# Key and value products of a cross attention made two stages earlier, layer norm statistics inside two loops, and two bias additions exchanged between TensorE and GpSimd, in a 12-stage decoder kernel

## The reference

```python
x = x + L0_attn(_layernorm(x), ...)
x = x + L0_xattn(_layernorm(x), ctx_2048, mask_Bx1xS2_ff0)
x = x + L0_ffn(_layernorm(x), ...)
x = x + L1_attn(_layernorm(x), ...)
x = x + L1_xattn(_layernorm(x), ctx_2048, ...)
...
# L0_xattn: x_dq, w_dq rounded through fp8 with one scale each
out = jnp.einsum('bmk,bkn->bmn', x_dq, w_dq) + bias        # bias: (4, 1, 256)
# L1_xattn, 16 heads of 16
q = x @ Wq + bq
kv = cond @ Wkv + bkv                                      # cond is ctx_2048
q, k = _fq_sym(q * scale, axis=-1), _fq_sym(k, axis=-1)    # rounded to 127 steps per token and head
v = _fq_sym(v, axis=2)                                     # one scale per column over all keys
attn = _fq_unsigned(softmax(q k^T))
return (attn @ v) @ Wp + bp
```

## Time and profile before

| | |
|---|---|
| median of 3 runs | 1985.23 us |
| the profiled execution | 1986.46 us, its span 1985.0 us |
| TensorE, VectorE, ScalarE, GpSimd busy | 78%, 62%, 41%, 35% of the span |
| L0a loop; L0x; L0f | from 63.8 us to 281; to 315; to 362 |
| L1a head, loop | to 382.5; to 637 |
| L1x head, loop | 641.5 to 710.5; to 933.5 |
| all stages behind | 933.5 to 1985 |

### The profile page before, as it was taken

The page is one execution under the profiler, slowest core; times in us unless marked ns, Lnnn a source line. Parts: engine busy times, 40 slices in busy tenths (PEclk is TensorE's granted clock), DMA queues, the critical chain, the costliest instruction groups (busy, mean ns, idle before and its releaser), DMA issues. The chain is left out here.

```text
span 1985.0 us, 26882 instructions
## 1 busy us (share of the span) xinstructions
PE 1538.4 (78%) x8607; PEld 1063.1 (54%) x8610; DVE 1237.6 (62%) x3228; ACT 817.1 (41%) x2164; POOL 702.2 (35%) x968
## 2 busy tenths in 40 slices
PE   4899964799998969996983892044687679948998
PEld 3566643688887513332662461012565469944665
DVE  3587776355555378886237327997788679953222
ACT  1244431244433277775225213212577458821111
POOL 1488840175663156664001003333555322210000
PEclk8799986899999755555986895567799979958999
DMA  5000002100000065554000002101000110000000
GB/s 197 22 7 7 1 12 90 41 7 1 6 1 1 0 106 91 89 90 115 28 1 0 1 1 87 37 0 54 1 1 1 73 57 2 2 0 1 0 0 22
DMA packets 98379, 62.20 MB, mean 31 GB/s; under 512 B 88896, under 2 KB 93376, under 8 KB 96448
## 3 DMA queue, kind: packets, MB, share of 16 engines
q1 hardware_dynamic: 98240, 60.48, 11.4%
HBM read 38.44 MB, written 1.05 MB: 20 GB/s over the span
## 5 line engine op out<-in xcount | busy, mean ns | idle before, releaser
L101 PE MATMUL banks<-arena_a,normed_t 128*128 128x512 f32 (+3 forms) x736 | 283.5, 535 | 11.7 <-PEq L2943 11.7
L421 POOL TENSOR_TENSOR lut_weights<-lut_weights,arena_b 128x536 f32<-128x536 f32 x128 | 179.2, 1400 | 193.4 <-DVE arena_b L411 183.5
L101 PEld LDWEIGHTS banks<-arena_a,normed_t 128*128 128x128 f32 x736 | 141.4, 212 | 123.9 <-issue 120.6
L580 POOL TENSOR_SCALAR work<-work,small 128x256 f32<-128x256 f32 (+1 forms) x384 | 178.1, 482 | 73.7 <-DVE small L572 73.7
L101 PE MATMUL banks<-arena_a 64*128 64x512 bf16 (+1 forms) x384 | 161.6, 539 | 17.8 <-ACT arena_a L1489 11.7
L1489 ACT ACTIVATE arena_a<-banks,work 128x1024 uint8<-128x1024 f32 x128 | 154.1, 1204 | 47.3 <-DVE work L1430 39.5
L1428 DVE TENSOR_REDUCE work<-banks 128x1 f32<-128x1024 f32 x128 | 155.3, 1214 | 26.9 <-PE banks L101 26.9
L1518 POOL TENSOR_SCALAR arena_a<-arena_a 128x1024 bf16<-128x1024 uint8 x128 | 133.1, 1045 | 90.0 <-DMA arena_a<-arena_a 84.8
L107 PE MATMUL banks<-identity,work 128*128 128x128 f32 x968 | 133.7, 279 | 16.8 <-DVE work L1086 11.2
L560 ACT ACTIVATE work<-banks,small 128x256 f32<-128x256 f32 (+1 forms) x258 | 115.2, 458 | 62.5 <-DVE small L547 58.4
L107 PEld LDWEIGHTS banks<-identity,work 128*128 128x128 f32 x968 | 113.3, 146 | 31.4 <-DVE work L1086 12.2
(11 more groups left out here) (407 smaller groups left out, 3437.8 us busy)
## 6 DMA issues: line engine op xcount, KB each, us to landing
arena_a<-in_L3f_wg SPq DMA_DIRECT2D x1, 4096.0 KB, 13.2
arena_b<-in_lut_idx SPq DMA_DIRECT2D x8, 268.0 KB, 2.8
arena_b<-in_L_wqn SPq DMA_DIRECT2D x1, 2048.0 KB, 12.4
arena_b<-in_L_wo SPq DMA_DIRECT2D x1, 2048.0 KB, 17.8
arena_a<-in_L_wq SPq DMA_DIRECT2D x1, 2048.0 KB, 7.5
arena_a<-in_L_wo SPq DMA_DIRECT2D x1, 2048.0 KB, 12.9
arena_a<-arena_a SPq DMA_TRANSPOSE x128, 2.4
arena_a<-in_L_wgu SPq DMA_DIRECT2D x1, 2048.0 KB, 9.7
```

What stands on the lines that cost most here:

```text
L101: ins = t.matmul(out, lhs_t, rhs, start=start and i == 0, stop=stop and i == n - 1)
L421: g.tensor_tensor(o, o, lut_t[j % 2], ALU.add).then_inc(*summed.up(c * LUT + j))
L580: ins = g.tensor_scalar(e[:, c], e[:, c], A.rl[n % 2][:, 2 * hh + i:2 * hh + i + 1], 0.0, ALU.mult, ALU.add)
```

## The change

- The values of L1x are made at the head of L0x (`cross_values_tensor` and `_scalar`), the keys in L0f: batch 0 ahead of its norm, batches 1 to 3 behind its low rank product (`cross_keys_tensor` and `_scalar`). They are kept in `W["vtf"]` and `W["k4"]` (in `work`). So that `work` is free for the keys, L1a's turned probabilities move from `work` to `big_b`.
- The loads of stage 4 are issued in L0a, between the mask's load and the first LUT chunk, no longer in L1a.
- L1x has no key or value products; VectorE reads the keys from SBUF, finds the values' scale behind batch 1's keys and rounds the values behind batch 0's queries; ScalarE rounds the values between the splits of batches 1 and 2.
- In both self attentions `statistics(b)` follows the last addition to batch `b` in the loop; the separate statistics and one barrier go.
- L0x: the addition on GpSimd goes. A one-row float32 matmul opens each tile's product (`row`, a row of ones times the inverse factor, made on VectorE, times a row of `bias1`), 8 in all.
- L1x's loop: the one-row product with `bp4` goes. GpSimd adds `bp4` to a tile of the residual at the fifth item of each 16.

```diff
@@ heads_product_vector
         v.tensor_tensor(x_of(b), A.bank01["y", m].f, x_of(b), ALU.add).then_inc(*out_added.up(A.s, m))
+        if m // 4 == GROUPS - 1:
+            v.wait_ge(*out_added.now())
+            statistics(b)
@@ l0_attention and l1_attention, vector
             yield MEET
-            for b in range(NB):
-                statistics(b)
-            yield MEET
@@ l0_attention, sync
             load(1)
+            load(4)
             yield from lut_sync(chunks)
@@ l0_cross, tensor
+            yield from cross_values_tensor(s)
+            t.wait_ge(*(yield loaded[1], "all"))
             for b in range(NB):
...
+                t.wait_ge(*(yield vs, s, "row"))
+                t.wait_ge(*(yield as_, s, "v", b))
                 t.wait_ge(*(yield xt_a, s, b))
                 for i in range(TB):
...
+                    t.matmul(o, row, W["bias1"][0:1, b * D:(b + 1) * D], start=True, stop=False)
+                    ins = products(t, o, [...], start=False)
@@ l0_cross, vector
-            v.wait_ge(*(yield gs, s, "bias"))
@@ l0_cross, scalar
             yield from norm_scalar(s, nf)
+            yield from cross_values_scalar(s)
@@ new, beside l0_cross
+    def cross_keys_tensor(s, b):
+        if b >= 2:
+            t.wait_ge(*(yield as_, s, "k", b - 2))
+        for i in range(TB):
+            ins = products(t, banks[6 + b % 2].f[:, i * D:(i + 1) * D], with_row(ctx_t, b, i, lambda k: W["wkv4"][:, k * 512:k * 512 + D], W["bk4"]))
+        ins.then_inc(*ts.up(s, "k", b))
+    def cross_keys_scalar(s, b):
+        a.wait_ge(*(yield ts, s, "k", b))
+        a.copy(W["k4"][:, b * CB:(b + 1) * CB], banks[6 + b % 2].f).then_inc(*as_.up(s, "k", b))
@@ l0_ffn, tensor
+            yield from cross_keys_tensor(s, 0)
             yield from norm_tensor(s, nf, low)
...
                 ins.then_inc(*ts.up(s, "low", b))
+            for b in range(1, NB):
+                yield from cross_keys_tensor(s, b)
...
+                    else:
+                        t.wait_ge(*(yield as_, s, "k", c + 2))
@@ l1_cross, tensor
-            for b in range(NB):
-                projected(banks[b].f, ctx_t, b, lambda k: W["wkv4"][:, k * 512:k * 512 + D], W["bk4"]).then_inc(*ts.up(s, "k", b))
...
-                    products(t, banks[z].f, [(W["wkv4"][...], ctx_t[...]) for kk in range(KH)]).then_inc(*ts.up(s, "v", z))
...
-                    products(t, out_bank(i)[:, 0:D], [(ot[i % 2][:, j * P:(j + 1) * P], wp[j]) for j in range(KH)] +
-                             [(ones[0:1, :], W["bp4"][0:1, :])]).then_inc(*out_made.up(s, i))
+                    products(t, out_bank(i)[:, 0:D], [(ot[i % 2][:, j * P:(j + 1) * P], wp[j]) for j in range(KH)]).then_inc(*out_made.up(s, i))
@@ l1_cross, scalar
                 as_.all(s, "split", b)
+                if b == 1:
+                    a.wait_ge(*(yield vs, s, "value_scale"))
+                    for k in range(KH):
+                        a.activation(v16[k], vtf[:, k * 1024:(k + 1) * 1024], ACT.Identity, scale=rv[:, k:k + 1]).then_inc(*as_.up(s, "rounded", k))
@@ l1_cross, gpsimd, in the loop
+                if n % H == 4:
+                    x_i = x[:, n // H * D:(n // H + 1) * D]
+                    g.tensor_tensor(x_i, x_i, W["bp4"], ALU.add).then_inc(*gs.up(s, "bias", n // H))
```

More of the change, by code:

```diff
@@ L932, in vector @@
             v.tensor_scalar(f, f, 1.0 / (FP8_MAX * FP8_MAX), None, ALU.mult).then_inc(*vs.up())
+            v.tensor_tensor(by_f, scale, ctx_scale, ALU.mult).then_inc(*vs.up())
+            v.wait_ge(*vs.now())
+            v.tensor_scalar(row, ones[0:1, :], by_f[0:1, :], None, ALU.mult).then_inc(*vs.up(s, "row"))
             for c in range(0, NB * CB, 1024):
@@ L1096, in scalar @@
             yield from norm_scalar(s, nf, low)
+            yield from cross_keys_scalar(s, 0)
             yield from gates_scalar(G_, s)
+            for b in range(1, NB):
+                yield from cross_keys_scalar(s, b)
             for b in range(NB):
@@ L1439, in vector @@
                 if (i := ended_at(n - 13)) is not None:
+                    v.wait_ge(*(yield gs, s, "bias", i))
                     v.wait_ge(*(yield out_made, s, i))
```

128 lines of the change are left out of this document (55 added, 73 removed).

## The result

The changed kernel takes 1956.26 us (median of 4 runs, 1954.65 to 1957.73) against 1985.57 us (4 runs, 1984.71 to 1988.39): a ratio of 0.9846, 95% interval 0.9834 to 0.9857, so 29.3 us less. The profiled execution took 1954.65 us, its span 1953.2; against the profiled one before the difference of the spans is 31.8 us.

A forecast was written before the change was run, and what follows sets the result against it. No engine was busy throughout; SyncE's last issue ended L1x's head and VectorE bound its loop. The terms summed to -28.6 us, 1957.9 for the profiled execution and 1957 us for the median, range 1950 to 1969.

The forecast's parts named there:

- head of L1x: L1x's head: turns start about 3.2 us in, so the last split ends at 31.6, not 54.9: -23.3 us (-25 to -21).
- bias rows in L1x's loop: L1x's loop: eight bias rows of 1.15 us no longer delay VectorE's scores or the last addition: -9.2 us (-9.2 to -6).
- contention with GpSimd's additions: L1x's loop: GpSimd's eight additions may each hold up a small VectorE operation: +1.0 us (0 to 5).
- end of L1a: End of L1a: one barrier and most of the tiles' statistics leave the stage's end: -3.3 us (-3.8 to -2.5).
- end of L0a: End of L0a: the same -3.3 us, less +2.1 for statistics delaying the drain: net -1.2 us (-3.3 to 0).
- start of L0a: Start of L0a: seven loads ahead of the first LUT chunk make SyncE issue later: +0.5 us (0 to 3).
- L0x: L0x: TensorE needs 4.43 us a batch with bias rows at the low clock, values hidden: +3.6 us (-2.8 to +4.5).
- L0f: L0f: keys ahead of turns cost +3.1 and +3.6, faster output products return 2.4 and 1: +3.3 us (+1 to +12).
- Rival 3: L1x's head: the chain does not start earlier because another wait replaces the turns; -5.3 us, 1980; chance 0.05.
- rival 1: L0x: the clock rises, L0x ends 2.8 us earlier than before, L0f's first keys begin fast; -37.7, 1947.5; chance 0.10.
- Rival 2: L0f: the keys run at the low clock, 18.8 us and not 10.1; -16.8 us in all, 1968.5; chance 0.12.
- rival 4: L1a's loop: value products reading both operands from `big_b` collide; at double time 60 us longer, 2017; chance 0.03.

The follow-up runs named there:

- e8: The change with the keys made in L1x again, behind the norm's turns and ahead of the queries, none in L0f: 1959.07 us.
- e12: The change with the keys made in L1x again, ahead of the norm's turns, none in L0f: 1975.61 us.
- e5: The change with the one-row product for bp4 back in L1x's loop and GpSimd's eight additions removed: 1964.59 us.
- e7: The change with each batch's statistics in the self attentions' loops issued one unit later: 1955.42 us.
- e1: The change with bias1 added by GpSimd again and the eight one-row matmuls in L0x removed, values still in L0x: 1951.68 us.
- e2: The change with L0x's bias rows out of the series, one 512-column row per batch, and two batches' turns ahead of their products: 1947.55 us.
- e3: The change with batch 0's keys made in L0x behind the values, not ahead of L0f's norm turns: 1952.60 us.
- e4: The change with batch 3's two key tiles moved behind L0f's first two output products: 1949.04 us.
- e11: The kernel before, unchanged, traced a second time: one profiled execution, 1990.12 us.
- e10: The change with the edits of e2, e3, e4 and e7 together, and ScalarE taking neighbouring batches' splitting steps in turn in L1x's head: 1933.43 us.
- e6: The change with each key transpose of L1x's head cut in two, halves of batches 0 and 1 issued early: 1953.19 us.

## Why the prediction was right, point by point

The forecast was 1957.0 us, the measurement 1956.3. Against the profiled execution the sum was -28.6 and the spans give -31.8. That the medians agree to 0.7 us is in part luck: the head of L1x brought 2.5 us more than forecast and the contention cost 1.0 less, L0x cost 1.3 more, and the profiled execution of the change was 1.6 us faster than its median. By the terms of the sum:

| term | predicted | measured | by |
|---|---|---|---|
| head of L1x | -23.3 | -25.8 | the change; e8, e12 |
| bias rows in L1x's loop | -9.2 | -9.1 | e5 |
| contention with GpSimd's additions | +1.0 | 0 | e5, the small operations of the loop |
| end of L1a | -3.3 | -3.4 | the change |
| end of L0a | -1.2 | -1.8 | the change; e7 |
| start of L0a | +0.5 | +0.4 | the change; within L0a's scatter |
| L0x | +3.6 | +4.9 | e1, e2 |
| L0f | +3.3 | +2.6 | e3, e4 |
| not in the sum: ahead of L0a's loop, and behind L1x | 0 | -1.0, +1.4 | scatter (the loop began 62.4 to 64.8 us in over all traces; e11) |

**The head of L1x.** The mechanism is the one predicted, link by link: turns at 3.2 us, chain of splits, SyncE last. Its size was 2.5 us short. The last split ended at 30.1 and not 31.6 us: the chain began 0.8 us earlier, at 7.3, and took 22.8 and not 23.5; SyncE needed 12.4 us behind it and not 13.4, which is the slow issue of before's one trace. Rival 3 falls with the head's length.

**L0x.** The stage came out at 34.3 us for 33.0. The step that was off is the 4.43 us of a batch: it took 4.61 (1.41 from the turn to the first row for 1.28, the rest 3.20 for 3.15), 0.7 us over four. The first turn (13.4 us in for 13.2), the last addition behind its product and the tail add 0.2 each. The clock was as predicted over the series; rival 1 falls. (By its own terms rival 1 ends L0x 2.6 us earlier than before, not 2.8; nothing hangs on it.) The values ran at 2.4 GHz, carried over from L0a.

**L0f.** Keys of batch 0: +3.1 for +3.1. The other keys ended where the sum had them, 10.0 us behind the low rank products, for 10.1; those products themselves took 0.4 less than before. The first output product gained 1.9 and not 2.4, the later ones 1.7 and not 1. With before's second trace the stage's price is nearer +2, since the clock moves L0f by more than a microsecond in either kernel. Rival 2 falls.

**L0a and L1a.** The end of L1a is as predicted. In L0a's drain the statistics cost 1.64 us (10.65 less 9.01) for the 2.1 in the sum. The two loops themselves are unchanged (253.3 us from L1a's first product to its last addition, 253.2 before), so rival 4 falls: two operands from `big_b` do not collide.

**Contention.** The prediction weighed a rule of the Trainium skill ("SBUF — State Buffer", Who interferes with whom) at up to 3.9 us more. Here a one-column `tensor_scalar` kept its 0.21 us beside GpSimd, where the two-column one of the earlier trace rows had taken 1.02. The same section says that a VectorE instruction with two inputs in SBUF contends with GpSimd's reads, and that one with at most one such input, outside the two-port modes, does not; both agree with the traces, the first in e1 (4.72 us for 1.22), the second in the loop, whose maxima read PSUM and took 1214 ns each as before. In which mode the one-column operation ran, no run here shows.

**The clock.** The prediction said that products and turns raised the clock and a stretch with many bias rows did not. In the heads of before and e12 that is what happened, and e8, whose keys ran at 1.00 once the turns stood ahead of them, does not contradict it. But that the rows are why L0x stayed at 1.2 GHz is not shown: e1 has no rows there and its turns and products were at 0.50 as well, with TensorE busy for half of the time. First e1, then the change:

```profile
297.15:309.80 12.65, 6.10 (x32) 3.43 (x32) 12.27 (x17) 2.34 (x4) 4.03 (x1) 0.50 0.00 1
```

```profile
296.80:315.20 18.40, 15.32 (x48) 6.88 (x48) 9.93 (x20) 2.34 (x4) 0.00 (x0) 0.50 0.00 1
```

So for L0x the price was right and its reason is open. By the rule of the Trainium skill ("TensorE: Matmul & The Clock Gate", Part 1), that sustained activity releases the throttle, e12's head should have been at 2.4 GHz; 23 us at 0.51 without a gap say otherwise. The same part has it as free to differ from run to run when a change comes, and L0f's 48.3 to 50.8 us agree.

## What to carry to other kernels

Ask of a product that is made early what it is put ahead of: reversing two blocks on TensorE was worth 13.8 us (by estimate 10.7 of it through the clock at which they then ran), where moving the keys out of the stage altogether brought 3. An addition to an engine's work is free in its waits and counts in full in the series, so put bias rows and independent products into the gap before a turn, not between a turn and what waits for it. When a chain is short enough, look at who follows it: here SyncE's nine transposes, 12.4 us behind the last split in the change, e8 and e10.

## What the runs showed of the hardware

- Key products with one-row matmuls were granted 1.2 GHz for 23 to 26 us without a gap when they stood ahead of the turns (before, e12), and 2.4 GHz for 29 us, queries included, behind them (e8): 3.15 against 1.68 us a tile.
- Behind 2.3 us at a barrier, TensorE began at 2.4 GHz and lost it after about 1 us of work without a gap, once in such products (e12, L1x) and twice in products without rows (e7 and e12, L0x); the latter got it back for their second half.
- TensorE's clock can be carried over a barrier: in the change L0x's values ran at 1.00 throughout after L0a, and work put behind them in the same wait did too (e2: 1.95 us for the rows of two batches, where one batch's took 2.07 later).
- A DMA transpose took SyncE 1.31 to 1.45 us at half the size (e6) and 1.38 at the whole (the change).
- GpSimd's addition stretched a VectorE operation with two inputs in SBUF from 1.22 to 4.72 us (e1), and its additions in L1x's loop left one-column operations at 211 to 216 ns (the change).
